# Cross-attention layer, one core: the scores for the row maxima half a step later, v's parts held twice by batch parity, p in six slots

## What is computed

```python
x = layer_norm(hidden_states, ln1_w, ln1_b)
q = x @ q_w + q_b;  k = ctx @ k_w + k_b;  v = ctx @ v_w + v_b      # heads of 32
scores = where(mask, einsum('bhqd,bhkd->bhqk', q, k) / sqrt(32), min)
out = einsum('bhqk,bhkd->bhqd', softmax(scores), v)
hidden = out @ cproj_w + cproj_b + hidden_states
y = gelu(layer_norm(hidden, ln2_w, ln2_b) @ fc_w + fc_b) @ proj_w + proj_b
return hidden + y
```

## Time and profile before

| what | value |
|---|---|
| median of 3 runs | 763.86 us (757.47 to 764.28) |
| the profiled execution | 761.63 us |
| its span, first to last instruction | 759.8 us |
| mean granted TensorE clock | 0.965 |
| PE busy | 701.7 us |
| DVE busy | 465.2 us |
| ACT busy | 321.7 us |
| POOL busy | 257.5 us |

### The profile page before, as it was taken

One profiled execution on the slowest core, in us unless ns is written; L12 is line 12 of the kernel. 1 busy time (PEld: TensorE's weight loads), 2 busy tenths in 40 slices (PEclk: granted clock), 3 DMA queues, 4 the chain that ended last, 5 costly groups with the idle time before them and its releaser, 6 DMA issues.

```text
span 759.8 us, 13142 instructions
## 1 busy us (share of the span) xinstructions
PE 701.7 (92%) x4544; PEld 607.5 (80%) x4544; DVE 465.2 (61%) x859; ACT 321.7 (42%) x582; POOL 257.5 (34%) x219
## 2 busy tenths in 40 slices
PE   3769989899998989899789999999999999999997
PEld 3658879798888879798677888888888888888886
DVE  5487978988789898978868775533225232252222
ACT  4146766867677776857751212112121121211110
POOL 6234656655546666556743121000000001000000
PEclk9787989999999999999889999999999999999999
DMA  7685554645455454434705400010001000010001
GB/s 222 158 239 149 161 159 123 166 141 156 139 155 153 140 155 138 113 114 142 196 1 161 130 1 1 15 41 1 1 0 56 0 0 0 0 55 1 1 0 57
DMA packets 51146, 69.16 MB, mean 91 GB/s; under 512 B 8344, under 2 KB 29208, under 8 KB 51104
## 3 DMA queue, kind: packets, MB, share of 16 engines
q1 hardware_dynamic: 50832, 68.07, 31.2%
q0 software_dynamic: 272, 0.54, 0.4%
HBM read 47.21 MB, written 20.99 MB: 90 GB/s over the span
## 4 chain that ended last, share of the span: by engine, by line
PE 70%; issue 9%; DVE 8%; POOL 6%; ACT 3%; DMA 3%; SPq 2%; DVEq 0%; ACTq 0%; POOLq 0%
PE psum L1212 8%; PE psum L1213 8%; PE psum L1214 8%; PE psum L1199 8%; PE psum L1198 8%; PE psum L1197 8%; PE psum L1004 6%; PE psum L1005 5%; PE psum L1006 5%; POOL p_lo L473 4%; PE psum L1038 2%; PE psum L1095 2%; DVE negm L755 2%; PE psum L1022 1%; PE psum L1116 1%
## 5 line engine op out<-in xcount | busy, mean ns | idle before, releaser
L473 POOL TENSOR_TENSOR p_lo<-p,p_hi 128x512 f16<-128x512 f32 x128 | 156.9, 1236 | 122.5 <-ACT p_hi L559 122.2
L685 ACT ACTIVATE h<-psum,cols 128x512 f32<-128x512 f32 x64 | 44.1, 689 | 290.0 <-PE psum L1199 290.0
L942 DVE CAST h_hi<-h 128x512 fp32r<-128x512 f32 x64 | 27.9, 436 | 208.1 <-ACT h L685 208.1
L557 ACT ACTIVATE p<-psum,maskbias 128x512 f32<-128x512 f32 x128 | 88.4, 690 | 45.8 <-PE psum L1022 44.8
L1212 PE MATMUL psum<-w_mlp,h_hi 128*128 128x512 f32 x256 | 100.7, 393 | 0.9 <-DVE hidden L784 0.9
L1214 PE MATMUL psum<-w_mlp,h_lo 128*128 128x512 f32 x256 | 99.7, 390 | 0.0
L1213 PE MATMUL psum<-w_mlp,h_hi 128*128 128x512 f32 x256 | 99.7, 389 | 0.0
L1197 PE MATMUL psum<-y_hi,w_mlp 128*128 128x512 f32 x256 | 99.7, 389 | 0.0
L1199 PE MATMUL psum<-y_hi,w_mlp 128*128 128x512 f32 x256 | 99.7, 389 | 0.0
L1198 PE MATMUL psum<-y_lo,w_mlp 128*128 128x512 f32 x256 | 99.6, 389 | 0.0
L559 ACT ACTIVATE p_hi<-psum,maskbias 128x512 f16<-128x512 f32 x128 | 88.8, 694 | 0.0
(11 more groups left out here) (105 smaller groups left out, 1516.1 us busy)
## 6 DMA issues: line engine op xcount, KB each, us to landing
qk_rows<-qk SPq DMA_DIRECT2D x32, 512.0 KB, 2.7
stacks<-qk_rows SPq DMA_DIRECT2D x64, 256.0 KB
stacks<-qk_rows SPq DMA_DIRECT2D x64, 128.0 KB
hidden<-in_x_dram SPq DMA_DIRECT2D x8, 512.0 KB, 4.5
ctx_sb<-in_ctx_dram SPq DMA_DIRECT2D x8, 512.0 KB, 5.2
w_mlp_raw<-in_L_xattn_fc_w_dram SPq DMA_DIRECT2D x16, 256.0 KB, 4.6
w_mlp_raw<-in_L_xattn_proj_w_dram SPq DMA_DIRECT2D x16, 256.0 KB, 6.2
out_dram<-hidden SPq DMA_DIRECT2D x16, 256.0 KB, 2.3
```

What stands on the lines that cost most here:

```text
L473: pool.tensor_tensor(p_lo[:, slot, :], p32[:, u % 2, :], p_hi[:, slot, :], ALU.subtract).then_inc(s["p_lo_done"], 1)
L557: act.activation(p32[:, u % 2, :], psum[:, ST + kc, :], ACT.Exp, bias=maskbias[:, kc:kc + 1], scale=SCALE32)
```

## The change

It does four things.
1. PE's scores of heads (0, 1) of group G+2 move to the end of the step, those of heads (2, 3) to the next step, right behind the first transposed_scores. VectorE's maxima follow: (2, 3) of group G+1 with the splitting pair behind low_parts (in step 0 behind the first context_lo), (0, 1) of group G+2 last. transpose_max moves from the front of the step to behind the projection, in step 3 to behind the last scores; ScalarE's maxima_out moves with it, to just before exps 2, in step 3 between exps 2 and 3. USES is reordered to match.
2. v's parts are held twice, for batches of even and odd number, in one tile per 128 context rows. The tile v1 goes; ScalarE writes the first part straight into vparts, and one of its three copies per batch is gone. The three instructions for v are made per half: first_part at the head of steps 2 and 3, rest_of_v on VectorE in steps 2 and 3, second_part on ScalarE in steps 2 and (next) 0, third_part on VectorE in step 2 ahead of add_values, and at the head of step 1. The hardware loop runs over pairs of batches, so that the parity q is known.
3. p_hi and p_lo have six slots, not eight: quarters 0 and 1 alternate by group, quarters 2 and 3 have one slot each and wait for the values of the group just before.
4. Rows and masks get other addresses, and the special order in the first step of the last batch goes.

```diff
-        USES = [("qk", 0), ("ctx", 0), ("ctx", 1), ("m", 0), ("c", 1),
-                ("qk", 1), ("m", 1), ("att", 0), ("att", 1), ("v", 0),
-                ("qk", 2), ("m", 2), ("v", 1),
-                ("qk", 3), ("m", 3), ("c", 0), ("x", 0), ("x", 1)]
+        USES = [("qk", 0), ("ctx", 0), ("ctx", 1), ("c", 1), ("m", 0),
+                ("qk", 1), ("att", 0), ("att", 1), ("v", 0), ("m", 1),
+                ("qk", 2), ("v", 1), ("m", 2),
+                ("qk", 3), ("c", 0), ("x", 0), ("m", 3), ("x", 1)]
+
+        def p_slot(g, u):
+            return (g % 2) * 2 + u if u < 2 else 2 + u
...
# POOL p_lo and ACT exps
-                        wait(pool, "pv_mm", (G - 1) * 2)
+                        wait(pool, "pv_mm", (G - 1 if u < 2 else G) * 2)
-                wait(act, "pv_mm", (G - 1) * 2)
+                wait(act, "pv_mm", (G - 1 if u < 2 else G) * 2)
...
# ACT
+            def first_part(b, kc, q):
+                wait(act, "v_added", b * 2 + (kc + 1))
+                wait(act, "pv_mm", (b - 1) * 8)
+                act.activation(vparts[q][kc][:, :, 1:1 + HD], v32[:, kc, :]..., ACT.Copy).then_inc(s["v1_cast"], 1)
+            def second_part(b, kc, q):
+                wait(act, "v_rest", b * 2 + (kc + 1))
+                act.activation(vparts[q][kc][:, :, 1 + HD:1 + 2 * HD], v32[:, kc, :]..., ACT.Copy).then_inc(s["v_cast"], 1)
...
# DVE
+            def rest_of_v(b, kc, q):
+                wait(dve, "v1_cast", b * 2 + (kc + 1))
+                dve.tensor_tensor(v, v, vparts[q][kc][:, :, 1:1 + HD], ALU.subtract).then_inc(s["v_rest"], 1)
+            def third_part(b, kc, q):
+                wait(dve, "v_cast", b * 2 + (kc + 1))
+                dve.tensor_tensor(vparts[q][kc][:, :, 1 + 2 * HD:VW], v32[:, kc, :]...,
+                                  vparts[q][kc][:, :, 1 + HD:1 + 2 * HD], ALU.subtract).then_inc(s["v_split"], 1)
...
# DVE step
+                if g == 1 and batch(it):
+                    third_part(it, 1, q)
                 low_parts(it, g)
...
                     context_lo(it, 0)
+                if g == 2 and batch(it + 1):
+                    rest_of_v(it + 1, 0, 1 - q)
+                maximum(it, g, (2, 3))
+                if g == 0 and batch(it + 1):
                     context_lo(it, 1)
                 if g == 3 and batch(it + 2):
                     normed_x(it + 2)
...
                     products_out(it, g)
-                maximum(it, g, (0, 1))
...
                     x_lo(it + 1)
-                    (third part of v, both halves)
...
                     statistics(b, [b * TT + t for t in range(TT)], "ln_stats", "ln_mv", "ln_var")
+                if g == 2 and batch(it + 1):
+                    third_part(it + 1, 0, 1 - q)
                 if g in (1, 2) and batch(it + 1):
                     add_values(it, g - 1)
+                if g == 3 and batch(it + 1):
+                    rest_of_v(it + 1, 1, 1 - q)
                 if g == 0 and batch(it - 2):
                     add_hidden(it, 1)
...
                     add_hidden(it, 0)
                 if g == 3 and batch(it + 2):
                     affine_x(it + 2)
-                    maximum(it, g, (2, 3))
-                if g == 3 and batch(it + 1):
-                    wait(dve, "v1_cast", it + 2)
-                    dve.tensor_tensor(v32[:, :, :], v32[:, :, :], v1[:, :, :], ALU.subtract).then_inc(s["v_rest"], 1)
+                maximum(it, g, (0, 1))
...
# PE step
                     transposes(it, "ctx", 0, it + 1, ctx_sb, "ctx_loaded", 16, "ctx_tr")
-                    values(it, g)
+                    scores(it, g, (2, 3))
+                    values(it, g, q)
                     transposes(it, "ctx", 1, it + 1, ctx_sb, "ctx_loaded", 16, "ctx_tr")
-                    scores(it, g, (0, 1))
+                    project_c(it, 1)
                     transpose_max(it, g)
...
-                    project_c(it, 1)
                 if g == 1:
-                    transpose_max(it, g)
-                    scores(it, g, (0, 1))
+                    scores(it, g, (2, 3))
                     for j in range(2):
                         transposes(it, "att", j, it - 1, att, "att_normed", 2, "att_tr")
-                    values(it, g)
+                    values(it, g, q)
                     project_v(it, 0)
+                    transpose_max(it, g)
...
                 if g == 2:
+                    scores(it, g, (2, 3))
+                    values(it, g, q)
+                    project_v(it, 1)
                     transpose_max(it, g)
...
                 if g == 3:
-                    transpose_max(it, g)
-                    values(it, g)
-                    scores(it, g, (0, 1))
+                    scores(it, g, (2, 3))
+                    values(it, g, q)
...
                     transposed_scores(it, g, 1)
...
+                scores(it, g, (0, 1))
                 if g == 3:
+                    transpose_max(it, g)
                     transposes(it, "x", 1, it + 2, xn, "x_normed", 2, "x_tr")
-                if not (last and g == 0):
-                    scores(it, g, (2, 3))
```

More of the change, by code:

```diff
@@ L227, in iterations @@
             for g in range(1, NG):
-                step(-1, g)
+                step(-1, g, 1)
             for it in (0, 1):
                 for g in range(NG):
[L231 to L234, removed]
+                    step(it, g, it % 2)
+            with eng.Fori(1, B // 2 - 1) as pair:
+                for q in range(2):
+                    for g in range(NG):
+                        step(pair * 2 + q, g, q)
             for it in (B - 2, B - 1, B):
                 for g in range(NG):
-                    step(it, g)
+                    step(it, g, it % 2)
                     if tail:
                         tail(it, g)
-            step(B + 1, 0)
+            step(B + 1, 0, 1)
         def chunks(eng, body):
@@ L626, in mask_columns, with step @@
                 act.activation(maskbias[:, :], maskcol[:, cut], ACT.Copy).then_inc(s["maskbias_ready"], 1)
-            def step(it, g):
+            def step(it, g, q):
                 if g == 0 and batch(it):
                     wait(act, "maskbias_ready", it + 1)
+                if g >= 2 and batch(it + 1):
+                    first_part(it + 1, g - 2, 1 - q)
                 qk_high(it, g)
@@ L640, in step @@
                     exps(it, g, 1)
-                    maxima_out(it, g)
-                    if batch(it + 1) and not (isinstance(it, int) and it == -1):
+                    if batch(it + 1):
                         x_hi(it + 1)
                     if batch(it):
-                        values_cast(it, 1)
+                        second_part(it, 1, q)
                 if g == 1:
                     exps(it, g, 0)
-                    maxima_out(it, g)
                     if batch(it - 1):
@@ L868, in step @@
                     products_out(it, g)
-                maximum(it, g, (0, 1))
-                if g == 0 and batch(it + 1) and not (isinstance(it, int) and it == -1):
+                if g == 0 and batch(it + 1):
                     x_lo(it + 1)
-                if g == 0 and batch(it):
-                    wait(dve, "v_cast", it * 2 + 1)
-                    for kc in range(KC):
-                        ins = dve.tensor_tensor(vparts[:, kc, :, 1 + 2 * HD:VW], v_heads[:, kc],
-                                                vparts[:, kc, :, 1 + HD:1 + 2 * HD], ALU.subtract)
-                    ins.then_inc(s["v_split"], 1)
                 if g == 1 and batch(it - 1):
@@ L904, in step @@
                     affine_x(it + 2)
-                if not last:
-                    maximum(it, g, (2, 3))
-                if g == 3 and batch(it + 1):
-                    wait(dve, "v1_cast", it + 2)
-                    dve.tensor_tensor(v32[:, :, :], v32[:, :, :], v1[:, :, :], ALU.subtract).then_inc(s["v_rest"], 1)
+                maximum(it, g, (0, 1))
             def weights(i):
@@ L1178, in step @@
                     transposes(it, "x", 0, it + 2, xn, "x_normed", 2, "x_tr")
-                if not (last and g in (0, 3)):
+                if not (last and g == 3):
                     transposed_scores(it, g, 1)
```

102 lines of the change are left out of this document (42 added, 60 removed).

## The result

The changed kernel takes 798.0 us in the median of 4 runs (796.4 to 800.0), the kernel before beside it 760.9 (757.5 to 764.3): 1.048 times as long, with an interval of 1.044 to 1.052. Forecast were 790 us, and slower.

The account below looks back on a forecast made before the run. PE was busy 92% of the span, and VectorE had only 5 us of air per batch. Four loop batches +19 us, iteration 1 +4, iteration 0 +1, iteration 6 +2, last batch +2.5: 28.5 on 761.6, so 790 us; range 762 to 812.

Parts of the forecast that it names:

- The forecast's chain: Attention: the new bank order puts VectorE's tail of each step on PE's path; 47.5 us a batch against 42.67, chance 0.52.
- Step 0: Attention loop: x_lo, the maxima's splitting pair and add_hidden precede the bank's release; 11.5 us taken, against 11.0 before.
- step 1: Attention loop: no wait for maxima, but the first project_v waits for VectorE to read att's bank; 11.6 us against 11.86.
- step 2: Attention loop: rest_of_v, the pair and third_part delay add_values; 12.4 us taken, a new 3.4 us wait before project_qk.
- Step 3: Attention loop: hidden_added, then transpose, ScalarE's copy and hand-overs precede the next project_qk; 12.0 us taken against 10.79.
- rival D: PE's clock drops with the longer waits, each batch running a few us at half rate: 800 to 812 us, chance 0.10.
- The start-up and iteration 0: Most of PE's 3.85 us start-up wait goes, -3.5 us, while steps 2 and 3 cost more: +1 us in all.
- the ring: In the attention, VectorE's tail holds back PE's project_qk through the banks, and VectorE's low_parts in turn wait for project_qk.
- iteration 1: First full loop pass: step 0 has no add_hidden, x_lo is the bound as before; +4 us.
- the last batch: No project_qk lies between the row of maxima and its reader; three steps see copy and DMA: +2.5 us.
- rival C: In steps 0 and 3 transposed_scores waits for the late row of maxima, 2 us twice a batch: 805 us, chance 0.15.
- Disturbance by POOL: VectorE's pair and third_part meet POOL's p_lo and may block: 50.8 us a batch if they exclude each other, else 44.5.

Follow-up runs that it names:

- two extra reductions: Changed kernel plus one unused 1.2 us VectorE reduction per batch in step 2, ahead of add_values or at the step's end: 809.7 us and 797.9 us.
- two kernels with later statistics: Changed kernel with step 2's statistics moved behind add_values, alone or together with third_part: 779.2 us and 774.3 us.
- v_twice_only: Kernel before plus v held twice, made per half, and six p slots; scores, maxima, transpose_max and bank order as before: 759.2 us, 0.997 times before.
- stats_late: Changed kernel with only the statistics of step 2 moved behind add_values: 779.2 us, 1.020 times before.
- scores_later_only: Changed kernel's order of scores, maxima, transpose_max and banks, with v and p as in the kernel before: 810.8 us, 1.064 times before.
- extra_ahead: Changed kernel with one unused VectorE reduction of 1.2 us per batch added in step 2 ahead of add_values: 809.7 us, 1.059 times before.

## Why the prediction was right

**The mechanism.** The forecast's chain was right in its links: the wait at project_qk of step 2 to 3 with the add of v as its releaser (forecast 3.4 us; measured 2.66 there, and 0.77 for the maxima in the same step, which the forecast did not have), the small ones at step 1 (hidden), before the first project_v (att_t) and no 1.70 before transpose_max. The two extra reductions and the two kernels with later statistics show the cause, not only the place; v_twice_only shows that the lateness of DVE alone costs nothing under the old order and its turns.

**The steps.** The steps took 10.99, 11.46, 12.82 and 13.42 us, against the forecast's 11.5, 11.6, 12.4 and 12.0. Step 0 came out below its lower end of 11.1, 1 a little under what I took, 2 a little over. Step 3 was missed beyond its upper end of 12.9, and 1.5 of its 13.42 us are the half clock behind the wait of step 2. *Here a term was left out:* "PE's clock I leave out ... more idling can only cost". It cost 1.5 us a batch, about 6 in the four batches, and with it rival D was in part true beside the forecast: the same wait brings both, and 798.0 lies nearer to the 800 at which D begins than to 790. Without it step 3 is 11.9, beside the 12.0 taken, and in stats_late, where the clock stayed at 1.00 in this batch, it took 11.94. The four steps together came to 48.69 us for the 47.5 of the sum, 1.2 more: -0.5, -0.1, +0.4 and +1.4.

The four batches in the loop made 22.6 us, not 19, and not the 24 of four times this batch. The batch that the sum starts from, 42.67, was a good one: those of before took 43.26, 44.27, 42.59 and 42.75 us. In iteration 3 the clock fell in the kernel before as well, behind the same 1.70 us of the earlier trace rows (the rows are under the last heading), and its step 1 took 13.49 us for 11.86. So "it is 1.00 in the batch read" was true of that batch and not of the loop.

**The start-up and iteration 0: the wrong term.** The sum had +1 for both, with -3.5 for the start-up wait of the earlier trace rows. Measured: iteration 0 starts 3.1 us late and ends 7.2 late. That term was mis-sized by 6 us, more than any other of the sum. The wait of 3.85 us is shorter, 0.58 at the same transposes, but others stand ahead of it, and one of 2.31 us (DVE's context low part) behind:

```profile
31.11 1.22 PE L1049 MATMUL psum<-stacks 97*128 97x256 f32 x4 [2.64 <-DMA stacks<-qk_rows]
...
35.54 0.55 PE L1015 MATMUL psum<-xs,w_att 128*128 128x256 f32 x1 [3.20 <-DVE v L794]
...
46.96 1.12 PE L1106 MATMUL psum<-ident,xn 128*128 128x128 f32 x4 [5.39 <-DVE xn L836]
...
55.68 0.63 PE L1106 MATMUL psum<-ident,ctx_sb 128*128 128x128 f32 x4 [0.58 <-DVE qk L802]
```

The second of them hangs on a load, and the third on what follows the second, as DVE's rows show:

```profile
32.42 1.29 DVE L774 BATCH_NORM_STATS2 stats<-hidden 128x6 f32<-128x512 f32 x2 [3.10 <-DMA hidden<-in_x_dram]
...
41.91 0.88 DVE L802 SCALAR_TENSOR_TENSOR qk<-psum,cols,qk 128x256 fp32r<-128x256 f32 x2 [5.32 <-ACT qk L597]
```

In the iteration before the first, the statistics wait for x of batch 1 to arrive; add_values stands behind them, and project_qk now waits for it, 3.20 us. This wait by itself doesn't put PE behind: it begins these matmuls at 35.54, where before began them at 37.10. The loss comes behind it. The matmuls run at half clock and take 5.26 us (35.54 to 40.80) for some 2.9:

```profile
35.54:41.10 5.56, 5.56 (x26) 5.56 (x27) 1.05 (x2) 0.59 (x2) 0.00 (x0) 0.50 0.66 177
```

The low parts of q and k come late in turn, DVE idles 5.32 us for them, and normed_x, queued behind them, the maxima and the pair, lets PE wait 5.39, where before waited 1.05 for it at 44.49. Step 3 of this iteration takes 14.47 us for 9.78. In iteration 0 the forecast's gain came, 3.1 us in step 0 for the 3.5, and so did the cost of step 2, 3.4 us; but step 3 takes 3.95 us more than before (13.20 for 9.25), where the sum had 1.2: PE waits for normed_x there too, 3.19 us at 94.24. I had read the ring in the loop and not in the start-up, where what is queued ahead of the release is a DMA. Of the rest, iteration 1 made +4.7 (4 forecast), iteration 6 +1.3 (2), the last batch +1.8 (2.5).

**The row of maxima (rival C).** Within the loop it is not behind any wait worth the name: of PE's waits for ACT's row (L605) the profile has four, 0.15 to 0.55 us, all at project_qk, whose bank that row frees. In the last batch, where no project_qk covers it, the DMA shows as forecast, in three steps with 1.82, 1.83 and 1.11 us; the first:

```profile
398.24 0.75 PE L1033 MATMUL psum<-stacks 99*128 99x256 f32 x4 [1.82 <-DMA stacks<-mrow]
```

**Disturbance by POOL.** The third parts of v and the pair did get less of it than before, and something else got it (shortest, median and longest in ns, then the times of the first and the last):

```profile
L764 DVE CAST m<-negm x32: 172/298/945, 45.5 to 410.5; 128x8 fp32r<-128x8 f32 x32
```

```profile
L816 DVE TENSOR_TENSOR vparts<-v,vparts x16: 664/686/1343, 34.1 to 400.5; 128x512 bf16<-128x512 f32 x16
```

The pair's first half has a median of 0.30 us for the 0.73 of the earlier trace rows (the mean of the pair together is 0.90 us; the forecast said over 0.6, but before it was 1.32, so this sign tells little), the third parts 0.69 for 1.53. But rest_of_v, which I put at 0.6 in step 2, took 1.49 at 271.23, beside POOL's add of the output bias:

```profile
269.64 2.52 POOL L492 TENSOR_TENSOR hidden<-hidden,cb_bc 128x512 f32 x2
```

So the sum of step 2 was right (12.4 forecast, 12.82) in part by luck, with two wrong terms in it that cancel: the third part, for which the value taken leaned to 1.53, measured 0.69, and rest_of_v, put at 0.6, measured 1.49. POOL's two adds end at 272.16, and DVE's 1.49 us end 0.56 after that, about the length that it has undisturbed. The Trainium skill ("SBUF — State Buffer", "Who interferes with whom") says that a VectorE instruction with two SBUF inputs and a GpSimd one that reads SBUF exclude each other: the trace agrees, with 0.69 us for this subtraction in the median and 1.49 here.

## What to carry to other kernels

Where uses of different kinds take turns in a shared buffer, the order of the turns decides whose queue ends on the critical path: write down, for each use, which instruction frees it and all that is queued ahead of that on its engine, in the start-up too. An instruction on an engine with spare time is free only behind the last release that somebody waits for; ahead of it, it costs nearly its whole length (1.13 of 1.21 us here), and what the clock takes besides. When a wait is cut, look for the next release in line: the batch came down from 48.7 us to 45.2 with two pieces moved past one release, and three more pieces moved past others brought only 0.3.

## What was not expected of the hardware

PE's clock did not follow the length of the waits alone. Behind the longest ones in the loop it fell every time. Over the 4.5 us behind the 2.66 us ahead of project_qk (in the kernel after), behind 3.75 (scores_later_only) and behind 3.79 (extra_ahead) its mean was 0.50 to 0.65: mostly or wholly at 1.2 GHz, where the rest of the batch has 2.4. The first of these cost about 1.5 us more than its own length, and where it was cut to 0.99 or 0.39 us both parts came back in the batch read: 1.67 us of wait and 3.15 us of batch in stats_late.

Behind shorter waits the clock fell in some batches and not in others, at the same place and behind the same wait. Behind the 2.03 us of scores_later_only the mean was 0.68, 1.00, 0.62 and 0.66 in iterations 2 to 5; behind the 0.98 to 0.99 us of stats_late 1.00, 0.64, 1.00 and 1.00; and behind the 1.70 us of the kernel before 1.00, 0.67, 1.00 and 1.00. In the three kernels with the old order and v twice, waits of 1.3 to 1.7 us brought no fall in iterations 1 to 5. What decides it between 1 and 2 us is not shown. Two windows of scores_later_only, each behind 2.03 us:

```profile
183.11:187.61 4.50, 4.50 (x27) 4.50 (x28) 1.06 (x2) 1.04 (x2) 2.29 (x3) 0.68 0.75 177
234.53:239.03 4.50, 4.50 (x48) 4.46 (x49) 1.45 (x3) 2.29 (x4) 2.29 (x3) 1.00 0.73 177
```

In the same 4.5 us the first has 27 of PE's matmuls and the second 48. Two windows of the kernel before, each behind 1.70 us (iterations 3 and 4):

```profile
193.44:197.94 4.50, 4.50 (x47) 4.28 (x48) 4.05 (x9) 2.73 (x5) 1.74 (x2) 0.67 0.33 127
237.64:242.14 4.50, 4.50 (x53) 4.10 (x54) 4.34 (x10) 2.62 (x5) 1.91 (x2) 1.00 0.31 122
```

So one batch is not enough to say what the clock does: the second pair of windows is the kernel that was read before the forecast, and the batch chosen there was one in which it stayed up.
